# Two-layer transformer block on one core: seven blocks of tokens normalised by activations on ScalarE instead of VectorE

## The reference

```
# layer 0, modulated by silu(cond) @ w_ada
x += g1 * self_attention_in_windows_of_128(ln(x) * (1 + sc1) + sh1)
q  = (ln(x) * (1 + sc2) + sh2) @ w_q                 # stage 2
x += g2 * attention_over_the_16_largest_scores(q, context of 154 tokens)
x += g3 * ((silu(a) * b) @ w_m2)   # a, b = (ln(x) * (1 + sc3) + sh3) @ w_m1, stage 3
# layer 1
x += self_attention_over_1024_tokens(ln(x) * g + b) + t1          # stage 4
x += masked_cross_attention(ln(x) * g + b, context) + t2          # stage 5
x += gelu((ln(x) * g + b) @ w1) @ w2 + t3                          # stage 6
ln(x) = (x - mean(x)) * rsqrt(var(x) + eps)
```

## Time and profile before

| | us |
|---|---|
| median of 3 runs | 1497.65 (1496.81 to 1498.06) |
| the profiled execution's own time | 1497.7 |
| its span, first to last instruction | 1495.9 |
| mean granted TensorE clock | 0.965 of full speed |
| PE busy | 1366.9 (91%) |
| DVE busy | 919.3 (61%) |
| ACT busy | 713.4 (48%) |
| POOL busy | 343.1 (23%) |

### The profile page before, as it was taken

The page is one execution under the profiler, slowest core; times in us unless marked ns, Lnnn a source line. Parts: engine busy times, 40 slices in busy tenths (PEclk is TensorE's granted clock), DMA queues, the critical chain, the costliest instruction groups (busy, mean ns, idle before and its releaser), DMA issues.

```text
span 1495.9 us, 25449 instructions
## 1 busy us (share of the span) xinstructions
PE 1366.9 (91%) x9100; PEld 683.0 (46%) x9100; DVE 919.3 (61%) x2815; ACT 713.4 (48%) x1454; POOL 343.1 (23%) x383
## 2 busy tenths in 40 slices
PE   7999887778889996989899999999999999988998
PEld 5467654434644553352224333333333335544675
DVE  3556498978788796765465666666676435550320
ACT  2344554565456353215544465555656664443221
POOL 1021078865655476010000000000000011010220
PEclk9999987989989999999999999999999999999999
DMA  5100003000000000000002000000000000000000
GB/s 192 44 29 26 20 19 114 10 1 1 4 12 1 29 2 27 1 1 1 1 1 71 2 1 2 1 2 2 1 12 1 2 2 2 14 5 1 15 20 26
DMA packets 22094, 26.75 MB, mean 18 GB/s; under 512 B 4205, under 2 KB 19635, under 8 KB 21709
## 3 DMA queue, kind: packets, MB, share of 16 engines
q1 hardware_dynamic: 21059, 25.03, 5.2%
q10 hardware_dynamic: 909, 0.10, 0.0%
HBM read 21.58 MB, written 3.08 MB: 16 GB/s over the span
## 4 chain that ended last, share of the span: by engine, by line
PE 76%; DVE 12%; issue 4%; ACT 4%; POOL 3%; DMA 0%; ACTq 0%; SPq 0%; POOLq 0%; DVEq 0%
PE bank L1082 27%; PE bank L1039 10%; PE bank L1122 8%; PE bank L1054 7%; PE bank L1018 6%; PE bank L997 3%; DVE x_hat L1501 2%; PE bank L976 2%; PE bank L1024 2%; PE bank L1146 2%; DVE left L1556 1%; PE bank L1165 1%; DVE left L1563 1%; PE bank L1004 1%; DVE stats L1488 1%
## 5 line engine op out<-in xcount | busy, mean ns | idle before, releaser
L1312 ACT ACTIVATE pr<-bank 128x512 f32<-128x512 f32 x656 | 353.4, 598 | 283.2 <-PE bank L1082 269.6
L1528 DVE TENSOR_REDUCE part_max<-bank 128x1 f32<-128x512 f32 x512 | 327.2, 685 | 180.7 <-PE bank L1082 180.2
L1082 PE MATMUL bank<-slot 32*128 32x512 f32 (+1 forms) x3072 | 387.2, 520 | 10.5 <-ACT pr L1312 6.1
L1082 PEld LDWEIGHTS bank<-slot 32*128 32x128 f32 x3072 | 160.8, 185 | 210.4 <-issue 158.6
L1578 POOL TENSOR_SCALAR var_eps<-mean_var 128x4 f32<-128x4 f32 x24 | 5.5, 229 | 906.9 <-DVE mean_var L1492 906.8
L1634 POOL TENSOR_SCALAR left<-left 128x308 f32<-128x308 f32 x128 | 125.5, 981 | 98.3 <-ACT exp_all L1334 43.3
L1122 PE MATMUL bank<-pr,v 128*17 128x512 f32 x1024 | 135.5, 601 | 0.2
L1039 PE MATMUL bank<-h_t,w_m 128*128 128x512 f32 x256 | 128.7, 629 | 4.4 <-DVE o_all L1472 3.2
L1636 POOL TENSOR_TENSOR probs<-left,exp_all 128x308 f32<-128x308 f32 x128 | 107.4, 839 | 10.7
L1553 DVE MAX8 top<-bank 128x8 f32<-128x154 f32 x256 | 69.5, 312 | 40.3 <-PE bank L1146 30.5
L1334 ACT ACTIVATE exp_all<-bank,neg 128x154 f32<-128x154 f32 x256 | 85.7, 387 | 10.6 <-DVE left L1556 6.8
(11 more groups left out here) (140 smaller groups left out, 1764.5 us busy)
## 6 DMA issues: line engine op xcount, KB each, us to landing
w_m<-in_L_xcond_w_m SPq DMA_DIRECT2D x1, 2048.0 KB, 9.0
w_m<-in_L_xcond_w_m SPq DMA_DIRECT2D x2, 1024.0 KB, 8.4
w<-in_L_xcond_w SPq DMA_DIRECT2D x2, 1024.0 KB, 6.5
w_ada<-in_L_xcond_w_ada SPq DMA_DIRECT2D x1, 1792.0 KB, 10.4
x_sb<-in_x SPq DMA_DIRECT2D x6, 256.0 KB, 7.3
res_row<-rows_dram SPq DMA_DIRECT2D x12, 128.0 KB, 3.5
out_x<-x_sb SPq DMA_DIRECT2D x6, 256.0 KB, 2.1
wa<-in_L_xcond_w_qkv SPq DMA_DIRECT2D x1, 768.0 KB, 7.1
```

The costliest lines, as they stand in the source:

```text
L1082: last = nc.tensor.matmul(g.bank(*tile)[:, into], left, right, start=True, stop=True)
L1312: nc.scalar.activation(m.pr[:, u % NPR, :], g.bank("s", gi, i)[:, :], ACT.Exp).then_inc(g.free("s", gi, i), 1)
L1528: nc.vector.tensor_reduce(m.part_max[:, slot, h * TB + i // 8, i // 4 % 2:i // 4 % 2 + 1], bank[:, :], axis=AX.X, op=ALU.max).then_inc(don ...
```

## The change

For the seven blocks the step x_hat is emitted by ACT instead of DVE: an Identity activation computes rstd * x + (-mean * rstd), with scale and bias from columns of four tiles each. POOL makes the bias with two more instructions in the step rstd, neg_mean = -1 * mean ahead of var_eps, and hat_bias = neg_mean * rstd behind rstd, with a semaphore of its own, scaled_done, which ACT's x_hat waits for. As DVE's did, it also waits until the last transposes of the block before it have read the buffer. The other blocks are as before. In `under`, x_hat is planned 0.5 of a unit behind its slot instead of 0.25.

The hunks are those of hat_on_act, `Plan.fill`, `under`, scalar_program (its x_hat), vector_program (x_hat) and gpsimd_program (rstd), in this order.

```diff
+def hat_on_act(s, b, n):
+
+    return (s, b) in ((2, 1), (3, 0), (4, 0)) or (s, b, n) == (3, 1, 0)
...
-                self.at(time + (later[0] if step[0] in SOON else later[1] if step[0] in LATE else 0.0), step)
+                self.at(time + (later[2] if step[0] == "x_hat" and len(later) > 2 else later[0] if step[0] in SOON else later[1] if step[0] in LATE else 0.0), step)
...
-        return plan.fill(slots, [A2 + (first + (i + aside) / per) * step for i in range(int((last - first) * per))], (0.25 * step, 0.9 * step))
+        return plan.fill(slots, [A2 + (first + (i + aside) / per) * step for i in range(int((last - first) * per))], (0.25 * step, 0.9 * step, 0.5 * step))
...
+        elif kind == "x_hat" and hat_on_act(step[1], step[2], step[3] // 2):
+            _, s, b, p = step
+            act.wait_ge(m.scaled_done, g.scaled[s, b, p // 2] + 1)
+            act.wait_ge(*g.ran("hat_turn", *g.h_order[g.h_index[s, b, p // 2] - 1], CK - 1))
+            for tt in range(2):
+                t = b * TB + 2 * p + tt
+                last = nc.scalar.activation(m.x_hat[:, p % 2 * 2 + tt, :], m.x[:, t, :], ACT.Identity, bias=m.hat_bias[:, t:t + 1],
+                                            scale=m.rstd[:, t:t + 1])
+            last.then_inc(m.hat_done, 1)
...
-        elif kind == "x_hat":
+        elif kind == "x_hat" and not hat_on_act(step[1], step[2], step[3] // 2):
...
+            if hat_on_act(s, b, n):
+                nc.gpsimd.tensor_scalar(m.neg_mean[:, t:t + 4], m.mean_var[:, t:t + 4, 0], -1.0, None, ALU.mult)
             nc.gpsimd.tensor_scalar(m.var_eps[:, t:t + 4], m.mean_var[:, t:t + 4, 1], 1e-6 if s <= 3 else 1e-5, None, ALU.add).then_inc(m.var_done, 1)
             pool.wait_ge(m.var_done, i + 1)
             nc.gpsimd.tensor_tensor(m.rstd[:, t:t + 4], m.var_eps[:, t:t + 4], m.power[:, :], ALU.pow).then_inc(m.rstd_done, 1)
+            if hat_on_act(s, b, n):
+                pool.wait_ge(m.rstd_done, i + 1)
+                nc.gpsimd.tensor_tensor(m.hat_bias[:, t:t + 4], m.neg_mean[:, t:t + 4], m.rstd[:, t:t + 4], ALU.mult).then_inc(m.scaled_done, 1)
```

More of the change, by code:

```diff
@@ L645, in memory @@
     m.rstd = sb("rstd", [P, B * TB])
+    m.neg_mean = sb("neg_mean", [P, B * TB])
+    m.hat_bias = sb("hat_bias", [P, B * TB])
     m.power = sb("power", [P, 4])
@@ L742, in memory @@
         sem(n) for n in ("silu_c_done", "silu_done", "o_copied", "neg_done", "all_done", "tails_copied"))
+    m.scaled_done = sem("scaled_done")
     m.ident_done, m.consts, m.var_done, m.rstd_done, m.row_added, m.out_gated, m.m2_gated, m.pick_done, m.mask_set, m.marked = (
@@ L766, in __init__ @@
         self.s_of = [step[1:] for step in plan.steps if step[0] == "s"]
+        on_act = [step[1:4] for step in plan.steps if step[0] == "rstd" and hat_on_act(*step[1:4])]
+        self.scaled = {key: i for i, key in enumerate(on_act)}
         self.o_order = [step[1:] for step in plan.steps if step[0] == "o_copy"]
```

## The result

| | before | changed |
|---|---|---|
| median, us | 1497.86 (1496.81 to 1499.18, 4 runs) | 1485.26 (1483.23 to 1487.26, 4 runs) |
| span of the profiled execution | 1495.9 | 1481.4 |
| mean granted TensorE clock | 0.965 | 0.966 |

The account below looks back on a forecast made before the run. No engine is full; DVE's work pays only where PE, 76% of the chain, waits for DVE. Terms 0 - 0.5 + 3.8 + 4.7 - 1.6 + 1.6 + 1.0 = 9.0 us took 1497.65 to 1488.7, range 1482 to 1496.5.

Parts of the forecast that it names:

- blocks 1 and 2: PE's lead: 0 at block 1 (-1.0 to +1.5), -0.5 us at block 2 (-1.2 to +0.5), with POOL 0.6 later.
- blocks 4 and 5: DVE gets 4.11 us back in each, shortening PE's waits; gain 4.7 us, between 2.3 (block 4 alone) and 6.7.
- the clock term: Matmuls after block 3's long wait run faster once its second wait is gone; up to 2.3 us, 1.0 taken.
- x_hat on ScalarE: Four x_hat in ACT's queue between neg and exp_all cost 1.92 us, 562 ns each; bounds 1.7 and 2.4.
- The pair on GpSimd: neg_mean and hat_bias on POOL, hat_bias near 0.23 us; with hand-overs the pair costs 0.6 us a block.
- that rival: hat_bias costs 1.04 us like rstd, so POOL takes back some 4.5 us, time 1493.2; chance 0.17.
- Block 3: PE's waits for x_hat (2.68) and o_all (4.01) shrink as DVE comes earlier; gain 3.8 us, bounds 2.5 and 5.06.
- Block 6: x_hat ahead of h_t in ACT's queue lengthens PE's wait for h_t; -1.6 us, between -3 and 0.
- Block 7: DVE gets 3.91 us back, the pick waits for ACT instead; PE gains 1.6 us, between 0 and 2.6.
- The slower rival: In ACT's in-order queue x_hat's wait and work delay exp_all; past about 4 us blocks 3, 4, 5, 7 give nothing; 1501.7; chance 0.08.
- The free port: Less DVE contention would also speed POOL's picks, some 6 us; time 1479 to 1482; chance 0.05.

Follow-up runs that it names:

- e3: Kernel before, with POOL making neg_mean and hat_bias unused in all seven blocks and x_hat still on DVE; ratio 1.0027 to the kernel before, +4.0 us.
- e6: Changed kernel with only block 7's x_hat on ACT, the other blocks on DVE; ratio 0.9999 to the kernel before, 0 us.
- e10: Changed kernel with only blocks 4 and 5 on ACT, the others' x_hat on DVE; ratio 0.9945 to the kernel before, -8.2 us.
- e9: Kernel before, with x_hat of blocks 3, 4 and 5 still on DVE but queued behind the next c_top; ratio 0.9942 to the kernel before, -8.7 us.
- e1: Changed kernel with block 6's x_hat back on DVE, the other six blocks on ACT; ratio 0.9905 to the kernel before, -14.2 us.
- e7: Changed kernel with each x_hat written twice on ACT, a wait between; ratio 1.0009 to the kernel before, +1.3 us.
- e2: Changed kernel with only blocks 3, 4 and 5 on ACT, the others' x_hat on DVE; ratio 0.9912 to the kernel before, -13.2 us.
- e4: The changed kernel timed once more, with nothing else altered; ratio 0.9915 to the kernel before, -12.7 us.

## Why the prediction was right, point by point

**The bound.** That DVE's work pays only where PE waits for DVE held. Of 24.6 us that DVE got back, PE's waits shrank by 14.3, in blocks 3, 4, 5 and 7, as named, some of them filled by slower matmuls.

**The sum.** 9.0 was forecast, and the two profiles lie 14.5 us apart. The 5.5 us that are missing are mainly blocks 1 and 2 (+4.3, nearly all clock, which had no term there) and blocks 4 and 5 (+2.4), less the 1.0 of the clock term. So the gain was put a third too low. That it stayed in the range is partly luck: the clock, which took and gave 2 to 4 us by place, added up to nearly nothing.

**x_hat on ScalarE.** 1.92 us for four was forecast, 2.07 measured, 592 ns each instead of 562. My slope came from rows with a PSUM source. Over seven blocks the error is 1.0 us. The Trainium skill, "VectorE: DVE Perf Modes", section "The TRN2 errata — SBUF-src ops pay a fixed extra latency per instruction", gives ScalarE 52 cycles more from SBUF than from PSUM, by which an estimate would be 605 ns. The trace, at 592, lies between, nearer to the page.

**The pair on GpSimd.** neg_mean 226 and hat_bias 202 ns; the choice of 0.23 over rstd's 1.04 was right, and that rival fell with the first look at the trace. Its cost in place I had put at nothing in block 1 and at 0.5 in block 2. e3, with the pair alone, was 4.0 us slower, but its trace shows the clock and no more waiting, so the pair's own cost isn't shown to be larger than that.

**Block 3.** 3.8 us of waits were forecast. At the transposes, which the forecast was about, 2.68 + 4.01 became 2.54, so 4.15 us ended. Over the whole stretch idle time fell by 6.6 and the clock took 2.6 back. The named waits came out right; that the stretch is 4.0 shorter too is partly luck, since its clock alone moved it by 3.3 us in e6. The timeline of POOL, ACT and PE at block 3 of the changed kernel:

```profile
301.68 1.04 POOL L1601 TENSOR_TENSOR rstd<-var_eps,power 128x4 f32<-128x4 f32 x1
...
302.79 0.20 POOL L1604 TENSOR_TENSOR hat_bias<-neg_mean,rstd 128x4 f32<-128x4 f32 x1
...
303.03 2.07 ACT L1306 ACTIVATE x_hat<-x_sb,hat_bias,rstd 128x256 f32<-128x256 f32 x4 [0.75 <-POOL hat_bias L1604]
...
305.25 1.76 PE L1014 MATMUL bank<-ident,x_hat 128*128 128x128 f32 x8 [2.54 <-ACT x_hat L1306]
...
309.89 3.27 PE L1049 MATMUL bank<-h_t,w_m 128*128 128x512 f32 x4
```

hat_bias ends at 302.99, x_hat waited 0.75 us for it, and all eight transposes run from 305.25 without the second wait. The clock's term had the wrong sign: I let the end of the long wait give back 1.0, and the four matmuls still took 3.27 us (3.77 in the earlier trace rows) while more work lay at the lower level.

**Blocks 4 and 5.** 4.7 forecast; 5.4 us of waits and 1.7 of clock, 7.1 in all, 8.2 by e10. The lower bound (block 4 alone) was far off, and the upper of 6.7 was passed because no clock was in it. PE's waits of 2.26, 2.42, 0.48 and 2.58 are gone; what it waits instead adds up to 2.36, of which this timeline of PE shows the parts before x_hat:

```profile
406.54 0.43 PE L1167 MATMUL bank<-ident,probs 128*32 128x128 f32 x8
...
408.80 0.66 PE L1014 MATMUL bank<-ident,x_hat 128*128 128x128 f32 x4 [0.28 <-DVE o_all L1491]
...
416.69 1.22 PE L1014 MATMUL bank<-ident,x_hat 128*128 128x128 f32 x8 [0.78 <-ACT x_hat L1306]
```

The transposes of block 4 start 7.5 us earlier than at 416.28 and those of block 5 take 1.22 us.

The first row had waited 2.26 us before, and there I misread. I took the wait for POOL's probs, as the row names it, but PE goes on at 411.26 and the picks of its own unit end at 409.26. In this timeline of ACT in the kernel before, the copy o_st, which these matmuls need as well, ends at 411.12:

```profile
410.43 0.20 ACT L1324 ACTIVATE neg<-top 128x2 f32<-128x2 f32 x1 [5.93 <-DVE top L1553]
410.54 0.58 ACT L1319 ACTIVATE o_st<-bank 128x512 f32<-128x512 f32 x1
```

It stood behind a neg that waited for the c_top behind x_hat on DVE. So this wait belonged to DVE's order, too, and e9 shows it: with c_top ahead of x_hat it is 0.46 us.

```profile
408.04 0.43 PE L1161 MATMUL bank<-ident,probs 128*32 128x128 f32 x8 [0.46 <-POOL probs L1640]
```

In the changed kernel it is gone, but only in part by that. PE itself came later there: the o_all and w_out matmuls at 394.25 and 398.84, partly at the lower level, took 4.9 us where they had taken 3.0.

**Block 6.** The term of -1.6 had the right sign and the wrong reason, so that it was nearly met (-2.2) is luck. PE's wait for h_t is 0.45 us, shorter than the 0.62 of the earlier trace rows, as the first row of this timeline of PE shows (changed kernel, blocks 6 and 7), and e1 shows that the loss stays without ACT:

```profile
524.38 1.96 PE L1028 MATMUL bank<-h_t,wa 128*128 128x512 f32 x4 [0.45 <-ACT h_t L1264]
...
560.89 1.41 PE L1014 MATMUL bank<-ident,x_hat 128*128 128x128 f32 x8 [3.25 <-ACT x_hat L1306]
...
567.83 0.43 PE L1167 MATMUL bank<-ident,probs 128*32 128x128 f32 x8 [1.49 <-POOL probs L1660]
...
571.78 0.58 PE L1167 MATMUL bank<-ident,probs 128*32 128x128 f32 x8 [1.87 <-POOL probs L1660]
```

**Block 7.** 1.6 forecast, 2.3 us of waits and -0.5 of clock in the trace. The second row is the transposes' wait for x_hat, 3.25 us. The fourth is the wait for POOL that I held for the limit, 1.87 where it was 1.56, and the third is a new one, 1.49, for the unit before it. What ended is the 4 us wait for o_all between the halves. By itself the block gives nothing that can be measured (e6).

**Blocks 1 and 2.** 0 and -0.5 forecast, and for the waits that is right: 0.2 us. The profile's 3.8 us are the clock, which I did not price there.

**The slower rival.** It did not happen, but its mechanism is real: in e7 the time is 1.3 us above before, where the rival said 4.0 (1501.7). Its threshold is not borne out. Wait and work on ACT pass 4.11 us there, and yet blocks 3, 4 and 5 don't fall to nothing (59.2 and 57.6 us against 60.2). My 0.08 for it was low, given that ACT's 47% was the only argument against, and e7 shows that this share says nothing.

**The free port.** It was no source of the gain. The first instruction of all 128 picks, durations min/median/max in ns, in the kernel before:

```profile
L1634 POOL TENSOR_SCALAR left<-left x128: 977/978/1157, 191.7 to 582.7; 128x308 f32<-128x308 f32 x128
```

And in the changed kernel:

```profile
L1658 POOL TENSOR_SCALAR left<-left x128: 976/977/999, 191.9 to 569.8; 128x308 f32<-128x308 f32 x128
```

One pick of the 128 took longer before, and it ran beside the x_hat of block 1 (216.90 to 219.05):

```profile
218.73 1.16 POOL L1634 TENSOR_SCALAR left<-left 128x308 f32<-128x308 f32 x1 [0.47 <-issue]
```

That is 0.18 us over the median; the 28 x_hat lost some 6 us over the 0.41 us that I took for one alone. The section "Who interferes with whom" of "SBUF — State Buffer" in the Trainium skill has DVE in its two-port mode and GpSimd exclude each other. Here nearly all of the cost shows on DVE's side.

**What the block list missed.** All of the gain was put down to DVE being relieved of x_hat. e9 shows that two thirds of what blocks 3 to 5 give (8.7 of 13.2 us, each uncertain by 2) can be had by moving x_hat a place down its own queue. I had the row for it, 7.03 us of waits for rstd, and treated it as a part of x_hat's cost, not as a second way to the same end.

## What to carry to other kernels

An in-order engine that waits for a short result of another engine costs its queue behind it, not only its own time: first try whether one independent step can stand between the producer and the waiter, and only then move work to another engine. An engine's idle share says nothing on whether a new step is on the chain; double the step and see whether the time follows (here 14.9 us for 15.8). Cut both traces at the same instructions and compare PE's busy and idle parts apart: it tells roughly a clock's gain, which need not last, from a wait's. Roughly, since slower matmuls fill waits; check it against a kernel that is unchanged at that place. And where a row names what an engine waited for, see whether that had ended long before or only after: the wait may be another's, as the 2.26 us of block 4 were ScalarE's copy and not GpSimd's pick.

## What the runs showed of the hardware

The lower clock level behind a wait did not follow the wait's length. Behind the same wait (2.82 us, 2.81 in e1) with the same matmuls, the clock over ten microseconds was 0.54 in the changed kernel, 0.53 in e1, and 1.00 in e2. Nor did it follow PE's idle time in a stretch: with less of it the clock was lower at block 3 (0.88 against 0.91) and higher at blocks 4 and 5 (0.94 against 0.89). It differs where nothing is changed: 0.84 in e6 and 0.91 before at block 3. Over the whole program the mean moved from 0.957 (e3) to 0.971 (e2), and of the same kernel two executions lay 4 us apart (1483.23 and 1487.26). So a change of 3 us in this kernel is not read from one profile. The clock may also have helped the timed gain: the five executions of e4 were granted 0.968 on average and the 17 of the kernel before beside them 0.963, and why is open. What sets the level's start and end is not settled by these runs.
